# A transformer layer with routed experts: the first loop's weight splits, modulation rows and projections are placed elsewhere

## What is computed

```python
mod = (silu(c) @ wmod).reshape(4, 6, 1, -1)
sa, ca, ga, sb, cb, gb = (mod[:, i] for i in range(6))      # ga, gb: size at least 0.25, sign kept
h = layernorm(x) * (1 + ca) + sa
q, k, v = split(h @ Wqkv.T + bqkv)
x = x + ga * (softmax(q @ k.T / 4, causal) @ v @ Wout.T + bout)
h = layernorm(x) * (1 + cb) + sb
# each token goes to its top expert, scaled by sigmoid(logit); a shared expert is added
x = x + gb * (shared(h) + routed(h))
```

## Time and profile before

| | us |
|---|---|
| median of 3 runs | 489.17 (488.92 to 491.56) |
| the profiled execution | 489.97 |
| its span | 488.2 |
| PE busy | 406.9 (83%) |
| DVE, ACT, POOL busy | 312.1, 229.1, 210.3 |

### The profile page before, as it was taken

One profiled execution on the slowest core, in us unless ns is written; L12 is line 12 of the kernel. 1 busy time (PEld: TensorE's weight loads), 2 busy tenths in 40 slices (PEclk: granted clock), 3 DMA queues, 4 the chain that ended last, 5 costly groups with the idle time before them and its releaser, 6 DMA issues.

```text
span 488.2 us, 8596 instructions
## 1 busy us (share of the span) xinstructions
PE 406.9 (83%) x3009; PEld 229.5 (47%) x3009; DVE 312.1 (64%) x635; ACT 229.1 (47%) x407; POOL 210.3 (43%) x251
## 2 busy tenths in 40 slices
PE   3787556588997788996997978899998999999991
PEld 3233123144454334543453525457555666666661
DVE  7765333586688896899996883487954444344441
ACT  2533142386766576674675672636231323323220
POOL 2482660237332675327823474310150455645332
PEclk9998697599999999999899998999999999999997
DMA  8467126875557945855244100499261234344210
GB/s 259 154 155 191 40 89 145 254 267 194 129 159 264 302 162 112 204 193 169 65 166 130 47 1 1 149 394 344 71 207 44 46 82 88 70 87 67 44 21 0
DMA packets 45921, 67.97 MB, mean 139 GB/s; under 512 B 5364, under 2 KB 33652, under 8 KB 45880
## 3 DMA queue, kind: packets, MB, share of 16 engines
q1 hardware_dynamic: 40200, 58.76, 39.2%
q0 software_dynamic: 5152, 8.14, 8.4%
q10 hardware_dynamic: 528, 0.52, 0.3%
HBM read 43.14 MB, written 25.18 MB: 140 GB/s over the span
## 4 chain that ended last, share of the span: by engine, by line
PE 52%; DVE 18%; POOL 11%; issue 6%; ACT 5%; DMA 5%; SPq 2%; ACTq 0%; DVEq 0%; POOLq 0%
PE bank L1486 35%; DVE mx L1122 4%; PE bank L1644 4%; PE bank L1628 3%; PE bank L1869 2%; POOL W L758 2%; DVE rowg L1223 2%; PE bank L1599 2%; ACT W L861 2%; DMA w_d<-rowg 1%; DMA mod_d<-h2T 1%; DMA qk_d<-W 1%; POOL rowg L765 1%; POOL W L739 1%; POOL rowg L766 1%
## 5 line engine op out<-in xcount | busy, mean ns | idle before, releaser
L886 ACT ACTIVATE W<-bank 128x512 f32<-128x512 f32 (+1 forms) x176 | 94.6, 563 | 59.1 <-PE bank L1628 57.5
L1486 PE MATMUL bank<-W 128*128 128x256 f16 (+2 forms) x756 | 108.8, 297 | 13.8 <-POOL W L732 6.3
L1122 DVE TENSOR_REDUCE mx<-bank 128x1 f32<-128x384 f32 (+3 forms) x176 | 104.8, 632 | 21.6 <-PE bank L1601 16.7
L1486 PEld LDWEIGHTS bank<-W 128*128 128x128 f16 x756 | 73.6, 100 | 49.0 <-issue 18.1
L758 POOL TENSOR_SCALAR_AFFINE_SELECT W<-W 128x512 f32<-128x512 f32 x64 | 47.1, 738 | 85.1 <-ACT W L886 85.0
L1628 PE MATMUL bank<-W 128*128 128x512 f16 (+3 forms) x256 | 65.1, 313 | 18.1 <-ACT W L886 12.7
L1486 PE MATMUL bank<-W,h2T 128*128 x276 | 67.1, 380 | 2.0 <-DVE W L1238 1.0
L829 POOL DMA_INDIRECT out<-h2T,sidx x23 | 36.3, 1578 | 64.7 <-DVE h2T L1456 64.3
L1599 PE MATMUL bank<-W 126*128 126x128 f16 (+3 forms) x208 | 54.5, 314 | 6.7 <-DVE mx L1122 6.7
L1644 PE MATMUL bank<-W 128*32 128x128 f32 (+3 forms) x512 | 48.9, 456 | 8.1 <-POOL W L758 8.1
L1628 PEld LDWEIGHTS bank<-W 128*128 128x128 f16 x256 | 22.1, 100 | 54.5 <-ACT W L886 26.6
(11 more groups left out here) (172 smaller groups left out, 546.7 us busy)
## 6 DMA issues: line engine op xcount, KB each, us to landing
w_d<-rowg SPq DMA_DIRECT2D x18, 512.0 KB, 4.3
W<-w_d SPq DMA_DIRECT2D x18, 512.0 KB, 8.0
stage<-in_gup SPq DMA_DIRECT2D x16, 512.0 KB
qk_d<-W SPq DMA_DIRECT2D x48, 128.0 KB
W<-qk_d SPq DMA_DIRECT2D x32, 192.0 KB, 4.5
stage<-in_down SPq DMA_DIRECT2D x8, 512.0 KB
x_sb<-in_x SPq DMA_DIRECT2D x4, 512.0 KB, 9.0
h_d<-gbb SPq DMA_DIRECT2D x4, 512.0 KB, 5.2
```

Of the source, the lines that this page charges most:

```text
L886: a.activation(PT[j][:, i:i + m, :], t_bank(N)[:, 0:m * w].rearrange("p (i n) -> p i n", i=m), ACT.Exp).then_inc(s_exp, 1)
L1122: v.tensor_reduce(mx_v[:, b % 2, hp0 // 4, par, i:i + m, t], s_bank(N)[:, 0:m * w].rearrange("p (i n) -> p i n", i=m), AX.X, ALU.max).then ...
L1486: i = t_.matmul(outp, l, r, start=(n == 0), stop=(n == len(prods) - 1), **kw)
```

## The change

- The first loop splits no weights; units 0 to 6 are split in loop b=0, one more than before, at steps 2, 6, 10, 15, 19, 23 and 28. SP writes units 0 to 2 after the modulation rows.
- PE computes part 0 of the modulation rows ahead of batch 0's projections, into T0, and part 1 at step 20. wmod comes in three pieces instead of two, and bqk ahead of wqkv with a semaphore of its own. POOL's two parts move from steps 30 and 36 of the first loop to steps 1 and 3 of b=0.
- The maxima's transpose (step 32) comes ahead of batch 1's turns (both at step 33). On SP its transfer goes ahead of the stage loads.
- Batch 1's projections alternate between M1 and M0, and the last two of the four are at steps 1 and 3 of b=0. `take_bank` waits for the last job on the same bank.
- Batch 0's v comes one or two steps earlier on PE (17 and 24), and DVE takes it at steps 21 and 28.

```diff
-SPLITS = {-1: {38: 0},
-          0: {1: 1, 4: 2, 9: 3, 14: 4, 19: 5, 23: 6},
+SPLITS = {-1: {},
+          0: {2: 0, 6: 1, 10: 2, 15: 3, 19: 4, 23: 5, 28: 6},
-FIRST = [(2, 4, 7), (7, 10, 13), (13, 15, 18)]
-HEAD = [(19, "v", 0, 0), (25, "v", 0, 1), (28, "turn", 1, 0), (30, "turn", 1, 1), (32, "max", 0, 0),
-        (34, "qk", 1, 0), (36, "qk", 1, 1), (39, "qk", 1, 2), (42, "qk", 1, 3)]
+FIRST = [(0, 3, 7), (7, 10, 13), (13, 15, 18)]
+HEAD = [(17, "v", 0, 0), (24, "v", 0, 1), (32, "max", 0, 0), (33, "turn", 1, 0), (33, "turn", 1, 1),
+        (39, "qk", 1, 0), (40, "qk", 1, 1)]
+NEXT = [(1, "qk", 1, 2), (3, "qk", 1, 3)]
@@ side_jobs
+    if b == 0:
+        jobs += [(job, c, part) for at, job, c, part in NEXT if at == n]
@@ side_bank
+            if c == 1 and job == "qk":
+                return [M1, M0][k % 2]
@@ sync
             sp.dma_start(wm[:, :, 0:2 * H], wmod_v[:, :, 0:2 * H]).then_inc(s_wm, 16)
+            sp.dma_start(bqk[:, :], bqkc).then_inc(s_bqk, 16)
             sp.dma_start(wq_s, wqkvT.rearrange("(k p) n -> p k n", p=P)).then_inc(s_wq, 16)
-            sp.dma_start(bqk[:, :], bqkc).then_inc(s_bias, 16)
+            sp.dma_start(wm[:, :, 2 * H:4 * H], wmod_v[:, :, 2 * H:4 * H]).then_inc(s_wmr[0], 16)
+            sp.dma_start(wm[:, :, 4 * H:6 * H], wmod_v[:, :, 4 * H:6 * H]).then_inc(s_wmr[1], 16)
...
-            sp.dma_start(wm[:, :, 2 * H:6 * H], wmod_v[:, :, 2 * H:6 * H]).then_inc(s_wmr, 16)
@@ sync
             stacks(0, 1)
+            maxima_out(0, 0)
+            maxima(0, 0)
             for k in range(3):
                 stage_load(k)
             qk_out(1, 0)
-            maxima_out(0, 0)
-            maxima(0, 0)
             stacks(1, 0)
             qk_out(1, 1)
             stacks(1, 1)
-            for k in range(2):
-                halves_out(k)
-                stage_load(k + 3)
             sp.wait_ge(s_m4, 1)
@@ gpsimd
-                    if b < 0 and n in (30, 36):
-                        modulation_rows(n == 36)
+                    if b == 0 and n in (1, 3):
+                        modulation_rows(n == 3)
@@ scalar
             h_parts(0, 1)
+            modulation_rows(0)
             for u in range(4):
                 qk_parts(0, u)
-                    if b < 0 and n == 16:
-                        modulation_rows(0)
@@ vector, v_out
+                if k == 0 and b == 0:
+                    ve.wait_ge(s_bias, 32)
@@ vector, the loops
+                    if b < 0 and n in (21, 28):
+                        v_out(0, n == 28)
@@ tensor, modulation_rows
-                if c == 0:
-                    pe.wait_ge(s_wmr, 16)
+                pe.wait_ge(s_wmr[c], 16)
+                if c == 1:
                     pe.wait_ge(s_q32, 2)
-                else:
-                    pe.wait_ge(s_mr, 1)
                 for k in range(KC):
-                    i = t_.matmul(M0[0:B, :], cs[:, 1, k], wm[:, k, 512 * (c + 1):512 * (c + 2)],
+                    i = t_.matmul([T0, M0][c][0:B, :], cs[:, 1, k], wm[:, k, 512 * (c + 1):512 * (c + 2)],
@@ tensor, take_bank
-                if last_job:
-                    pe.wait_ge(*released(*last_job[-1]))
+                used = [j for j in last_job if side_bank(*j) is side_bank(job, c, k)]
+                if (job, c, k) == ("qk", 1, 1):
+                    pe.wait_ge(s_mr, 2)
+                elif used:
+                    pe.wait_ge(*released(*used[-1]))
@@ tensor, turn_out
-                if G:
-                    pe.wait_ge(s_nrm, G)
+                pe.wait_ge(*((s_nrm, G) if G else (s_q32, 8)))
@@ tensor, before the loops and in them
             pe.wait_ge(s_h32, KC)
+            modulation_rows(0)
             for u in range(4):
                 project_qk(0, u)
-                    if b < 0 and n in (14, 20):
-                        modulation_rows(n == 20)
+                    if b < 0 and n == 20:
+                        modulation_rows(1)
```

More of the change, by code:

```diff
@@ L302, in build @@
         s_wm = sem("s_wm")
-        s_wmr = sem("s_wmr")
+        s_wmr = [sem(f"s_wmr{r}") for r in range(2)]
+        s_bqk = sem("s_bqk")
         s_wq = sem("s_wq")
@@ L746, in bias_x @@
                 if b == 0:
-                    po.wait_ge(s_bias, 48)
+                    po.wait_ge(s_bias, 32)
                 link(g.tensor_tensor(bga, boutb, bc[:, b % 2, 0:H], ALU.mult))
@@ L952, in hidden_high @@
                 a.activation(hT[:, 0, n % FC], hid[:, n % 2], ACT.Copy).then_inc(s_hh, 1)
[L954 to L957, removed]
             def modulation_rows(c):
@@ L962, in modulation_rows @@
                     ac.wait_ge(s_wl, 1)
-                a.activation(mraw[:, 512 * c:512 * (c + 1)], M0[0:B, :], ACT.Copy).then_inc(s_mr, 1)
+                a.activation(mraw[:, 512 * c:512 * (c + 1)], [T0, M0][c][0:B, :], ACT.Copy).then_inc(s_mr, 1)
+            h_parts(0, 0)
+            h_parts(0, 1)
+            modulation_rows(0)
+            for u in range(4):
+                qk_parts(0, u)
             def query_parity(c):
@@ L1095, in modulation_columns @@
                 ve.wait_ge(s_mc, 1)
-                ve.wait_ge(s_bias, 48)
+                ve.wait_ge(s_bqk, 16)
                 v.tensor_copy(sac[:, :, :], T2[:, 0:8].rearrange("p (k b) -> p k b", k=KC))
@@ L1313, in _ @@
                             negate(c, k)
-                        elif job == "v":
+                        elif job == "v" and c:
                             v_out(c, k)
@@ L1550, in scores_apart @@
                     pe.wait_ge(s_col, 1)
+                    pe.wait_ge(s_mr, 1)
                     pe.wait_ge(s_qz, 3)
```

## The result

| us | before | after |
|---|---|---|
| median of 20 runs | 490.52 | 494.76 |
| the profiled execution | 489.97 | 495.28 |
| its span | 488.2 | 493.5 |
| mean granted clock of TensorE | 0.952 | 0.940 |

The change makes the kernel slower: the ratio of after to before is 1.0062, 95% interval 1.0035 to 1.009, which is 3.0 us (1.7 to 4.4). The ratio compares means, and one execution of before, at 607 us, and one of after, at 496.4, count as slow and are not in it. The 20 runs of after do not lie in one heap: ten are from 495.3 to 496.4 us and the profiled one (495.28) is the lowest of them, the others from 488.8 to 494.3. So the trace, in which 5.3 us are lost, shows the dearer half of the executions; what it says of places and mechanisms holds, its sum is larger than the ratio.

A forecast was written before the change was run, and what follows sets the result against it. It took the waits on SP's queue before the first weight write, from 66 to 102 us, as the bound. 4.9 gained less 0.7, 3.7 and 0.3 left 0.2 us, so 489.0 us was forecast, range 483.0 to 493.0.

The forecast's parts named there:

- the forecast's signs of being wrong: Hole ending under 89 or over 95 us, no wait at the boundary of b=1, or later loops changing their length.
- rival D: First loop ends slow, POOL's rows become the wait, first weight write issued at 89 us: slower, 493 us; chance 0.25.
- gain at unit 11: In b=0 ACT's split wait moves from n=4 to n=10; unit 11 starts at 93.5 instead of 98.36, 4.9 us gained.
- So POOL is through with (1,1): End of first loop: POOL finishes low half (1,1) between 55.8 and 58.5 us, taken as 57.0, clock between the levels.
- The chain behind it: From 57.0 us: POOL's moved rows to 73.1, SP's queue to the weight write at 85.2, landing 7.12 us, to 92.4.
- My upper sum by the rule: POOL's rows beside two DVE splits in b=0: held the whole 1.23 us for each, making the sum 1.0 us later.
- The boundary: Weight unit 6 split at n=28, written ahead of the maxima: PE's first unit of b=1 3.7 us later, bounds 0 to 5.3.
- PE's idling of 4 us may lower its clock again: Start of b=1, after PE's wait for the maxima: a loss of 0 to 2 us, taken as 0.3.
- Behind the hole of b=0: Units 11 to 16 of b=0 meet PE's lower clock after the split wait: minus 0.7 us, between nothing and 2.
- From there the same lines, shifted: After the start of b=1 the later loops were to keep their own length; no gain or loss was priced there.
- B: Shorter chain to the first weight write (landing 4.3, small write 2.3) and only 2 us wait at b=1: 482.3 us; chance 0.31.
- C: The split wait in b=0 disappears, unit 11 starting at 76 instead of 98.4: some 472 us; chance 0.04.

The follow-up runs named there:

- Experiment 7: After plus dummy matmuls of constants, read by nobody, where PE idles in the first loop: ratio to before 0.9993, 489.94 us.
- Experiment 2: Before with only the split of weight unit 6 moved from step 23 to step 28 of b=0: ratio to before 1.0155.
- experiment 1: After with SP writing weight unit 6 behind the second batch's q, k and maxima instead of ahead of them: ratio to before 0.9963.
- experiment 3: After with both parts of POOL's modulation rows at step 22 of the first loop instead of steps 1 and 3 of b=0: ratio to before 1.0001.
- experiment 4: After with the edits of experiment 1 and experiment 3 together: ratio to before 0.9863.
- experiment 5: Experiment 4 with SP writing the modulation rows ahead of the second batch's q and k: ratio to before 0.9783, 479.82 us.
- experiment 6: Experiment 5 with SP writing weight units 0 and 1 behind the second batch's last q and k writes, ahead of the stacks: ratio to before 0.9696, 475.73 us.
- experiment 8: After with the edits of experiment 1 and Experiment 7 together: ratio to before 0.9847, 484.06 us.
- experiment 9: Experiment 6 with the dummy matmuls of Experiment 7 in its first loop: ratio to before 0.961, 472.07 us.

## Why the prediction was wrong

The forecast was 489.0 us with a range of 483 to 493 and 0.25 for slower. It is slower and beyond the range: 494.76 by the median. (By the ratio, on the forecast's own scale, it is 492.2, inside the range and still the wrong way.) Two of the forecast's signs of being wrong came: the hole ended at 95.7, over 95 us, and the later loops changed their length. The case that came is rival D by its place and its numbers: it wanted a first weight write issued at 89 us and unit 11 at 97.3; they came at 88.37 and 96.65, past its point of 87.7. That its numbers fit is in part luck. D had 1.5 us from the first loop and the rest from splits that block POOL for their full length and from late landings; the first loop gave 4.3, and the stretch from there to unit 11 was 1.1 us shorter than in my sum. And D had nothing beyond 3.7 us for the boundary, where 5.9 were lost.

| step | forecast | after | dummies (7) |
|---|---|---|---|
| maxima negated | 43.2 | 44.8 | 43.5 |
| last units of the first loop on PE | 50.4 | 53.5 | 50.8 |
| POOL through with (1,1) | 57.0 | 61.3 | 56.1 |
| last low half | 73.1 | 77.2 | 71.9 |
| first weight write issued | 85.2 | 88.4 | 83.0 |
| unit 11 | 93.5 | 96.65 | 91.2 |
| gain at unit 11 | 4.9 | 1.7 | 7.2 |

*The step that failed* is "So POOL is through with (1,1) between 55.8 and 58.5; I take 57.0, since the clock here is between the levels". It came at 61.3, outside its own bounds. I had moved work and left the clock of the first loop where the trace of before had it. With the splits gone from it and the modulation rows ahead, PE had a different pattern of holes, and the granted clock fell twice: to .52 from 28 to 34 us, where before has 1.00, and to .53 from 48 to 59. The maxima came 1.6 us late, the last units another 1.5, and the projections, which I priced between the levels, took the lower one in full: 1.2. Experiment 7 shows how much of it is the clock: with the clock kept these three points come 1.3, 2.7 and 5.2 us earlier than in after. A hold of DVE of 1 us, told of last, lies ahead of the last units in both. The same two stretches in before, against .52 and .53:

```profile
28.00:34.00 6.00, 5.74 (x55) 2.89 (x52) 2.73 (x6) 0.73 (x2) 5.75 (x11) 1.00 0.68 143
48.00:59.00 11.00, 4.95 (x32) 1.35 (x25) 4.57 (x10) 1.78 (x3) 6.34 (x8) 0.66 0.21 73
```

The .66 was there to be read; but the row also shows PE busy for 4.95 of 11 us, in waits that the change was to remove. With the clock kept the chain to (1,1) is 0.9 us ahead of the forecast. And I had called it a gain that DVE would no longer idle at 31.45 and 34.05; it idled there 1.28 and 1.98 us for PE, which was on the lower level now; with the clock kept it was 0.32 and 0.71.

*The chain behind it* was priced well. POOL's rows with mask and two low halves: 15.9 us against 16.1. SP from the last low half to the weight write: 11.2 against 12.1 (q and k landed 2.2 us after their last issue where I had 4.0; the rows' write took 5.09 where I had 4.3). The landing: 7.24 against 7.12. Part 0 of the modulation rows took PE 3.24 us (15.18 to 18.42), inside my 1.9 to 3.8.

Beside DVE's two low halves of the splits one row operation took 1.93 us instead of 1.06, another 1.34 instead of 0.72, and the first of the splits 1.72 instead of 1.22:

```profile
65.82 1.93 POOL L724 TENSOR_SCALAR h2T<-h2T 4x256 f32<-4x256 f32 x1
...
72.08 1.34 POOL L723 TENSOR_TENSOR h2T<-h2T 4x256 f32<-4x256 f32 x1
73.50 1.06 POOL L724 TENSOR_SCALAR h2T<-h2T 4x256 f32<-4x256 f32 x1
```

```profile
65.10 1.72 DVE L1228 SCALAR_TENSOR_TENSOR rowg<-stage,rowg 128x1024 f16<-128x1024 f32 x1 [1.60 <-ACT rowg L940]
...
71.62 1.22 DVE L1228 SCALAR_TENSOR_TENSOR rowg<-stage,rowg 128x1024 f16<-128x1024 f32 x1
```

That is 0.9 and 0.6 on POOL, 1.5 us for the two, against 1.4 in my sum. The rule of the Trainium skill ("SBUF — State Buffer", "Who interferes with whom"), that the two engines exclude each other for a whole instruction, agrees with these rows: the first split, at 65.10, came while POOL's operation of 65.02 to 65.74 ran and was 0.5 us longer, POOL's next one came at 65.82 and ends about its own length after the split's end (66.82), and the one at 72.08 about its own length after the second split's end (72.84). My upper sum by the rule had POOL held for a split's full length, and that wasn't reached: each time it came when the split had run for 0.5 to 0.7 us.

*The boundary.* PE's first unit of b=1 was forecast 3.7 us later, and counted from the end of b=0 its first matmul came 3.9 later. The step behind it, "PE's idling of 4 us may lower its clock again: 0 to 2 us, I take 0.3", was mis-sized: 2.0, 0.2 of it at the first unit and 1.8 by (1,4). Experiment 2 says the same, 1.5 us behind a wait of 4.5. Why 0.3? I had no reason but that such losses had seemed small; the rows, 2.72 against 1.47, spoke for the upper end, for units which PE computes back to back.

*Behind the hole of b=0* I took 0.7 for the clock and the trace shows 0.8.

*The far end.* I had forecast "From there the same lines, shifted". At (3,36) 1.1 us are lost again, in a stretch where the granted clock of after is .65 and .83 (296 to 302 and 302 to 310 us) and that of before .82 and 1.00. No instruction there is the change's, and experiments 1 and 3 to 8 show the like, of 1.0 to 1.2 us; experiment 2, which is before but for one step, and experiment 9 don't. The cause stays open.

*Together.* From 0.2 us gained to 5.3 lost in the profiled execution: 3.2 at unit 11 (4.3 in the first loop less 1.1 behind it), 1.9 at the boundary, 1.1 in b=3, 0.1 behind the hole, less 0.9 of small gains behind (1,4) and behind the last exp unit.

*A reading.* In the earlier trace rows I gave slice 7 of PE a 5; it is a 6, and the 5 is slice 8. Nothing was worked out from it.

*Rivals.* B was wrong for its reasons: the two transfers that it wanted shorter took 7.24 us (it had 4.3) and 5.09 (it had 2.3), and the boundary lost more and not less. The transfer that was shorter, q and k's, it didn't name. C named the right target and held it impossible in SP's order. That was right for the change, and experiment 6 shows what the order was worth: unit 11 at 77.0, as C had it (76), and 475.7 us where C had 472, though ACT's wait shrank to 5.2 us and didn't disappear.

## What to carry to other kernels

Price an edit at the clock that its own pattern of work will get, not at that of the trace before: where the engine's holes move, keep both levels for every matmul up to the next transfer, and put the lower one into the sum when the stretch is on the chain. A wait of 4 to 5 us of PE cost the wait and 1.1 to 2.0 us more (after and experiments 2, 3 and 7). And before work is moved off a queue's critical stretch, write down the queue's whole list with the time at which each entry's data are ready: in experiment 3 a 16 KB write that could go at 51 us stood behind entries of 77 us, two 512 KB ones behind it, and putting these three in order of readiness took the ratio from 0.9863 to 0.9696, 8 us.

## What was not expected of the hardware

More matmuls made the kernel faster: 5.5 us at unit 11 for dummies whose results nobody reads. With them the granted clock was 1.00 all through 28 to 62 us, where it had twice fallen to .50. Whether a dip comes later in its place varies: 1.6 us near (1,20) in experiments 1, 4 and 7 and none in 3, 5 and 9.

POOL and DVE held each other up, and not only where I had counted it. A DVE operation on 16 columns took 1.12 us in after beside a low half on POOL, which itself took 1.73 instead of 1.15; in before, at 52.7 us, the same operation took 0.15:

```profile
47.10 0.67 DVE L1114 SCALAR_TENSOR_TENSOR W<-h2T,W 128x512 f16<-128x512 f32 x1
47.70 1.12 DVE L1115 SCALAR_TENSOR_TENSOR rw<-rw_s,rw 128x16 f16<-128x16 f32 x1
```

```profile
47.06 1.73 POOL L736 TENSOR_TENSOR W<-W 128x512 f16<-128x512 f32 x1 [12.43 <-ACT W L865]
49.26 1.15 POOL L736 TENSOR_TENSOR W<-W 128x512 f16<-128x512 f32 x1 [0.46 <-ACT W L865]
```

These rows too read as one engine at a time: POOL's 1.73 end about 1.1 us after the first DVE operation, and DVE's small one ends with them, at 48.8. It stands on the chain of after (47.77, 1.05 us there), ahead of the last maxima of the first loop, and so 1 us of the lateness at 53.5 is its own. Experiment 7 has the same hold (46.39, 1.12 us), so what it gains on after is not this.
